# A fused attention and FP4 feed-forward layer on one core: the down projection's half chunk carries the weights' high and low parts, 17 matmuls a tile in place of 18

## The reference, cut to what matters

```
gate = fp4_linear(x, w_gate)          # 256 -> 704
y    = fp4_linear(x, w_up)            # 256 -> 704
h    = silu(gate) * y
out  = fp4_linear(h, w_down)          # 704 -> 256
```

## Time and profile before

| | |
|---|---|
| median of 3 runs | 763.99 us (763.69 to 764.46) |
| the profiled execution, its time | 763.37 us |
| its span, first to last instruction | 761.6 us |
| mean granted TensorE clock | 0.982 |
| PE busy | 718.2 us, 94% |
| DVE, ACT, POOL busy | 616.5, 581.2, 559.8 us |
| PE share of the chain that ended last | 84% |

### The profile page before, as it was taken

The page is one execution under the profiler, slowest core; times in us unless marked ns, Lnnn a source line. Parts: engine busy times, 40 slices in busy tenths (PEclk is TensorE's granted clock), DMA queues, the critical chain, the costliest instruction groups (busy, mean ns, idle before and its releaser), DMA issues.

```text
span 761.6 us, 17047 instructions
## 1 busy us (share of the span) xinstructions
PE 718.2 (94%) x4964; PEld 687.4 (90%) x4964; DVE 616.5 (81%) x1402; ACT 581.2 (76%) x1547; POOL 559.8 (73%) x585
## 2 busy tenths in 40 slices
PE   4999999999999968699999999999999999999983
PEld 3899999999999857699999999999999999999983
DVE  5988788889888985788878878788799887898773
ACT  3577776777898887468887877767777788888887
POOL 4677677677667675758887878878888788787761
PEclk9999999999999988799999999999999999999998
DMA  4222222222222110000000000000000001111113
GB/s 131 70 67 75 83 76 72 71 65 77 78 69 77 49 28 1 1 1 2 1 2 1 2 1 2 2 2 1 1 1 2 15 29 44 43 43 36 49 64 131
DMA packets 39767, 29.80 MB, mean 39 GB/s; under 512 B 3446, under 2 KB 39676, under 8 KB 39676
## 3 DMA queue, kind: packets, MB, share of 16 engines
q1 hardware_dynamic: 37228, 26.50, 11.5%
q10 hardware_dynamic: 2448, 2.23, 1.1%
HBM read 20.32 MB, written 8.39 MB: 38 GB/s over the span
## 4 chain that ended last, share of the span: by engine, by line
PE 84%; issue 5%; DVE 4%; POOL 3%; ACT 2%; DMA 1%; ACTq 0%; SPq 0%; POOLq 0%; DVEq 0%
PE bank L856 63%; PE wide L856 5%; PE wide L959 5%; PE bank L918 3%; PE bank L864 3%; PE bank L916 2%; PE bank L966 2%; PE wide L905 2%; POOL scratch L387 1%; ACT scratch L488 1%; POOL scratch L373 1%; DMA scratch<-L_attn_Wv 1%; PE wide L892 0%; POOL scratch L430 0%; POOL scratch L423 0%
## 5 line engine op out<-in xcount | busy, mean ns | idle before, releaser
L856 PE MATMUL bank<-wf_hi,rounded 128*128 128x352 f32 (+1 forms) x1792 | 405.1, 311 | 14.2 <-DVE wf_lo L739 6.1
L856 PEld LDWEIGHTS bank<-wf_hi,rounded 128*128 128x128 f32 x1792 | 302.7, 191 | 17.5 <-DVE wf_lo L739 6.3
L856 PE MATMUL bank<-wf_lo,rounded 128*128 128x352 f32 (+1 forms) x896 | 275.2, 307 | 0.0
L856 PEld LDWEIGHTS bank<-wf_lo,rounded 128*128 128x128 f32 x896 | 171.4, 191 | 0.0
L430 POOL TENSOR_TENSOR scratch<-scratch 128x704 f32<-128x704 f32 x64 | 94.9, 1482 | 78.5 <-DVE scratch L812 75.1
L856 PE MATMUL bank<-qkv_hi,rounded 128*128 128x512 f32 (+1 forms) x512 | 145.9, 339 | 0.0
L415 POOL TENSOR_TENSOR scratch<-scratch 128x704 bf16<-128x704 f32 x64 | 99.3, 1551 | 14.5 <-ACT scratch L609 14.0
L856 PEld LDWEIGHTS bank<-qkv_hi,rounded 128*128 128x128 f32 x512 | 93.3, 191 | 9.9
L781 DVE TENSOR_TENSOR scratch<-scratch,bank 128x352 f32<-128x352 f32 x64 | 33.2, 519 | 72.2 <-ACT scratch L566 70.1
L435 POOL TENSOR_TENSOR scratch<-scratch 128x704 f32<-128x704 bf16 x64 | 89.0, 1390 | 0.7 <-DVE scratch L816 0.7
L373 POOL TENSOR_TENSOR scratch<-scratch 128x512 f32<-128x512 f32 x64 | 68.0, 1063 | 27.8 <-DVE scratch L726 27.5
(11 more groups left out here) (100 smaller groups left out, 1578.2 us busy)
## 6 DMA issues: line engine op xcount, KB each, us to landing
scratch<-x_feat SPq DMA_DIRECT2D x64, 128.0 KB, 2.2
scratch<-x_tok SPq DMA_DIRECT2D x64, 128.0 KB, 2.1
out<-scratch SPq DMA_DIRECT2D x64, 128.0 KB, 1.7
scratch<-w_ffn ACTq DMA_DIRECT2D x17, 128.0 KB, 2.2
scratch<-L_attn_Wq SPq DMA_DIRECT2D x1, 256.0 KB, 3.0
scratch<-L_attn_Wk SPq DMA_DIRECT2D x1, 256.0 KB, 3.1
scratch<-L_attn_Wv SPq DMA_DIRECT2D x1, 256.0 KB, 3.9
wo<-L_attn_Wo SPq DMA_DIRECT2D x1, 256.0 KB, 3.1
```

The costliest lines, as they stand in the source:

```text
L856: last = pe.matmul(dst, x(c), w(c), start=first and n == 0, stop=n == len(terms) - 1)
```

## The change

A constant `TAIL = 64` is added, the rows of the last half chunk. The rows 64 to 127 of the last chunk, zeros before, are filled: on the weights' side `wf_hi` gets the low part of the same 64 weight rows there, on the activations' side `hqt_hi` gets a second copy of the 64 high rows. One matmul over 128 rows then gives hi x hi and hi x lo together, and a matmul over 64 rows gives lo x hi. Four places change.

- PE: 15 matmuls for the five full chunks, one over all 128 rows of the last, and one over its first 64 rows: 17 in place of 18.
- ACT, every tile: L584 becomes three activations: 64 x 128 from rows 0 to 63 to rows 64 to 127, 64 x 128 in place, and 128 x 640 for the five full chunks.
- DVE, pieces 16 and 17 alone: L739 becomes two subtractions, 128 x 128 to `wf_lo` and 64 x 128 to the lower half of `wf_hi`.
- ACT's DMA issues, pieces 16 and 17 alone: two DMAs in place of one, so that the tail's 64 columns of `w_raw` are a second copy of the 64 before them; the semaphore count that DVE waits for follows.

```
+    TAIL = I % P
...
-                        act.dma_start(w_raw, w_ffn.rearrange("j p n -> (j p) n")[bass.ds((i + 1) * P, P), :]
-                                      ).then_inc(ld_w, 16)
+                        if i + 1 < NW - KC:
+                            act.dma_start(w_raw, w_ffn[i + 1, :, :]).then_inc(ld_w, 16)
+                        else:
+                            act.dma_start(w_raw[:, 0:D - TAIL], w_ffn[i + 1, :, 0:D - TAIL]).then_inc(ld_w, 16)
+                            act.dma_start(w_raw[:, D - TAIL:D], w_ffn[i + 1, :, D - P:D - TAIL]).then_inc(ld_w, 16)
...
-                        act.activation(hqt_hi[b1][:, :, :], wide[:, 0:IP].rearrange("p (c n) -> p c n", c=IC),
+                        act.activation(hqt_hi[b1][TAIL:P, IC - 1, :], wide[0:TAIL, (IC - 1) * P:IP], ACT.Copy)
+                        act.activation(hqt_hi[b1][0:TAIL, IC - 1, :], wide[0:TAIL, (IC - 1) * P:IP], ACT.Copy)
+                        act.activation(hqt_hi[b1][:, 0:IC - 1, :],
+                                       wide[:, 0:(IC - 1) * P].rearrange("p (c n) -> p c n", c=IC - 1),
                                        ACT.Copy).then_inc(h_hi, 1)
...
-                        dve.tensor_tensor(wf_lo[:, :, bass.ds((i - 1) * P, P)],
-                                          w_bank(i)[:, 0:D].rearrange("p (c n) -> p c n", c=KC),
-                                          wf_hi[:, :, bass.ds((i - 1) * P, P)].bitcast(F32),
-                                          ALU.subtract).then_inc(w_los, 1)
+                        piece = bass.ds((i - 1) * P, P)
+                        if i - 1 < NW - KC:
+                            dve.tensor_tensor(wf_lo[:, :, piece],
+                                              w_bank(i)[:, 0:D].rearrange("p (c n) -> p c n", c=KC),
+                                              wf_hi[:, :, piece].bitcast(F32), ALU.subtract).then_inc(w_los, 1)
+                        else:
+                            dve.tensor_tensor(wf_lo[:, 0, piece], w_bank(i)[:, 0:P], wf_hi[:, 0, piece].bitcast(F32),
+                                              ALU.subtract)
+                            dve.tensor_tensor(wf_hi[TAIL:P, 1, piece], w_bank(i)[TAIL:P, P:D],
+                                              wf_hi[TAIL:P, 1, piece].bitcast(F32), ALU.subtract).then_inc(w_los, 1)
...
                         three(pd[:, 0:D], lambda c: hqt_hi[b][:, c, :], lambda c: hqt_lo[b][:, c, :],
-                              down(wf_hi), down(wf_lo), IC).then_inc(d_s, 1)
+                              down(wf_hi), down(wf_lo), IC - 1, last=False)
+                        pe.matmul(pd[:, 0:D], hqt_hi[b][:, IC - 1, :], down(wf_hi)(IC - 1), start=False, stop=False)
+                        pe.matmul(pd[:, 0:D], hqt_lo[b][0:TAIL, IC - 1, :], down(wf_hi)(IC - 1)[0:TAIL],
+                                  start=False, stop=True).then_inc(d_s, 1)
```

More of the change, by code:

```diff
@@ L68, in layer_kernel @@
     HALF = I // 2
+    TAIL = I % P
+    assert 2 * TAIL == P
     NB = I // BLK
@@ L684, in attention @@
                     if t == 3 and live_seq(i, 1, NW):
-                        need(dve, ld_w, 16 * (i + 2))
+                        need(dve, ld_w, 16 * (i + 2 + max(0, i + 2 - NW + KC)))
                         need(dve, w_scs, i + 1)
@@ L850, in _, with three @@
         def _(pe):
-            def three(dst, x_hi_ap, x_lo_ap, w_hi_ap, w_lo_ap, chunks, first=True):
+            def three(dst, x_hi_ap, x_lo_ap, w_hi_ap, w_lo_ap, chunks, first=True, last=True):
                 terms = [(x, w, c) for c in range(chunks)
@@ L855, in three @@
                 for n, (x, w, c) in enumerate(terms):
-                    last = pe.matmul(dst, x(c), w(c), start=first and n == 0, stop=n == len(terms) - 1)
-                return last
+                    op = pe.matmul(dst, x(c), w(c), start=first and n == 0, stop=last and n == len(terms) - 1)
+                return op
             pe.wait_ge(consts, 3)
```

## The result

The changed kernel takes 780.72 us (median of 4 runs, 779.99 to 782.24), the kernel before 763.84 us (4 runs). The ratio is 1.0223, 95% interval 1.0205 to 1.0241. The prediction of 758.8 us (756.4 to 766.0) had the wrong sign. The profiled execution of the changed kernel took 779.99 us with a span of 778.3 us, 16.7 us longer than the span before.

What follows compares the result with a forecast made beforehand. PE's rate of starting matmuls was taken to bound the kernel. Terms -6.0 (one matmul less), +0.2 (split copy), +0.5 (last tiles) and +0.1 (weights) gave -5.2 us on 763.99: 758.8 us, range 756.4 to 766.

Steps and rivals of the forecast that it cites:

- PE holds the step and one matmul is worth 0.119 us: In 6.85 us feed-forward steps, PE's matmul starts set the pace; one fewer saves 0.119 us in 50.5 steps, 6.0 us.
- The steps that DVE holds: In the two layer-norm stretches, DVE sets steps of 6.92 to 6.94 us; five and three steps gain nothing, plus 0.5 beside.
- I take nothing, since the transposes' change is of type and operand layout and this one is only of a row count.: At both switches between 128-row and 64-row matmuls on PE: cost taken as 0, between bounds of 0 and 0.16 us each.
- The rival: Both row switches around the 64-row matmul cost the full overlap, 0.16 us each: about +12 us, 776 us; chance 0.15.
- ACT's copy in three: L584 split on ACT: 0.3 us more a tile (bounds 0.21 and 0.43), mostly hidden; 0.2 us lost in second layer-norm stretch.
- the check against load: ACT's densest stretch: 5.87 us of work a step, 6.2 with the split copy, under the new step of 6.73 us.
- The rival in which ACT becomes the holder: Split copy costing about 1 us more makes ACT hold 16 or so two-normalisation steps: about 762 us; chance 0.10.
- Weights and DMAs: At PE's wait for weight piece 17: two subtractions for one add about 0.1 us; the extra DMA is hidden.
- The last tiles: After the last `gate_up(1)`, ACT's queue leads: two longer copies less one shorter down projection lose 0.5 us (0.3 to 0.75).

## Why the prediction was wrong, point by point

- **PE holds the step and one matmul is worth 0.119 us.** Right. The run with nothing but 17 matmuls over full rows has 6.73 us in the plain steps, as computed, and 759.28 us in all against a sum that without ACT's part gives 758 to 759. The steps that DVE holds kept their 6.9 to 7.0 us, as counted. In the profiled execution the 56 steps from 346.96 to 725.66 us take 378.7 us, 5.7 us less than before. But 0.8 us more is spent ahead of them and 1.0 us more behind the last `gate_up(1)`, for which the sum had no term once the split is gone.
- **"I take nothing, since the transposes' change is of type and operand layout and this one is only of a row count."** This is the step that failed. The price was a choice between bounds of 0 and 0.16 us a border, and the choice fell on the bound that no row supported, while the nearest row (0.08 us behind the transposes) and the rule cited from the Trainium skill ("TensorEngine Tiling (Array Packing)", Key Properties) both spoke against it. The runs show 0.19 to 0.20 us a border, above the upper bound: the border costs not only the overlap of its first matmul (0.09 us) but also its successor's (0.10 to 0.11 us). Twice 0.20 less 0.12 is 0.28 us more a step, where 0.12 less was forecast, and over some 60 steps that turns -5.2 into +17. By its outcome the rule that changing the tiling mode drains TensorE agrees with the trace: 64 rows cost, 96 rows don't, and 64-row matmuls in a row pay once. The drain itself is not seen in the rows.
- **The rival** had the mechanism, its place and its sign, with a chance of 0.15 and 776 us; it was 4.7 us short, by 0.04 us a border. The range left it out. It was a known case of the other sign with nothing but its price unknown, and deserved far more.
- **ACT's copy in three.** 0.33 us in the plain steps against 0.3 taken: right, and hidden there. In ACT's unbroken rows it is 0.48 us, above the upper bound of 0.43. And the check against load (5.87 us a step and room up to 6.73) was the wrong one: what counts is the loop through ACT, DVE and POOL, which is 6.97 us a step with the split. Had the borders been free, the split would have cost 3.8 us (759.28 to 763.08; 3.2 by the ratios), not 0.2 + 0.5. The rival in which ACT becomes the holder had the right stretch, but set its threshold by load, at 0.86 us extra a tile; 0.48 us was enough. In the changed kernel itself none of this shows, since PE's 7.13 us is longer than the loop.
- **Weights and DMAs.** PE's wait on the last piece is 6.3 us, it was 6.1; 0.1 was predicted.
- **The last tiles.** From the transposes behind the last `gate_up(1)` to the end of the span it is 27.3 us (778.3 - 751.01); before it was 26.3 us (761.6 - 735.33). 0.5 us more was predicted (0.3 to 0.75), 1.0 measured. The run without the split has 27.2 us too (757.5 - 730.26), so the longer copies were not shown to be the cause, and what is stays open.

## What to carry to other kernels

Before a matmul is removed by packing, look whether the packed form changes the row count to 64 beside 128-row neighbours; here each such border cost more than the matmul that was saved, and it was cheaper to fill the unused rows with something harmless (zeros, or the low parts' own product) and stay at 128. If 64-row matmuls are needed, put them next to one another. And to judge whether an added operation is hidden, add up the loop through the engines over as many steps as its pattern has, in the stretch with the most side work, rather than an engine's busy share.

## What the runs showed that was not expected

- A border between 128 and 64 rows costs 0.19 to 0.20 us at full clock, in both directions and in each of the places tried; 96 rows cost nothing, and the border behind the transposes adds to it.
- An activation over 64 partitions is not overlapped with the 128-partition one ahead of it (0.47 us from start to start against 0.34), nor with a second one over the other 64 partitions (0.28 us for 0.27 us records), shifted or not; behind the second, the next one starts after 0.17 us. Why was not tried.
- DVE's copy of 64 x 128 words within SBUF took 0.22 us by itself and 0.60 us (up to 0.84) where it started beside a running POOL operation: it ended 0.07 to 0.09 us after that operation. What such a copy costs depends on what is left of POOL's running operation.
